# A decoder layer with attention, a long convolution and routed experts: the convolution by blocks of 128, and expert rows kept in a region per expert

## The chip, the cores and the metric

The kernel runs on one core of one Trainium2 chip. The metric is the device time of one execution in microseconds (us). Three runs of the kernel before took 780.53, 782.09 and 788.21 us; the median is 782.09. The profile comes from one execution whose page gives a span (first to last instruction) of 786.9 us and no other time.

## The reference

`x` is 4 batches of 512 tokens by 128 values. Three parts follow one another, each added to its input and normalised over the 128 values (mean and variance, no scale):

1. **Attention**: 16 heads of 8 values, 4 key and value heads, RMS norm and rotary turn of q and k, scores capped by `50*tanh(s/50)`, causal softmax, output projection.
2. **Cross attention, convolution, feed-forward**: a softmax over 32 context rows gives `c_t`; from it come scales and shifts. The scaled, normalised input goes through `s4d`, a causal convolution over 512 positions, one kernel `K[d, 0..511]` per value (by FFT of length 1024 in the reference), plus `x*D_skip`. Then a second scale and shift, a norm, a feed-forward of 512 hidden values with exact GELU, and a norm.
3. **Experts**: `gates = x @ rW + rb`; the 2 best of 8 experts are taken per token, weighted by a softmax over the two gates; each expert is `gelu(x @ W1 + b1) @ W2 + b2` with 512 hidden values. Two shared experts run on all tokens and are averaged. `out = norm(x + shared + sum_e w_e * y_e)`.

Everything is float32 and the output is (4, 512, 128).

## The kernel before, in words

**The order.** Every engine walks the same written order. `iterate` has 7 iterations `i`, each of 8 head pairs `p`, each of 6 slots `n`. In iterations 0 to 3 the slots hold the score products of batch `i` (`fill`), with the value products and the copy of their result (`close`, `oT`) at the end of a pair, and the token products (`tokens`) in its third slot. Into these slots `STEPS` puts the steps of earlier batches: `(after, p, n, name)` runs at pair `p`, slot `n` of iteration `b + after`. So batch 0's cross attention runs in iteration 1, its convolution's inverse part and feed-forward in iteration 2, its norm, gates, ranks and row numbers in iteration 3. `ONCE` holds steps that run once (convolution taps and their transform). `UNIT_AT` puts the first 43 expert units into iterations 4 to 6; the rest (`moe`) follows. An engine that waits in one step holds up all that stands behind it in its order.

**Convolution.** The taps K (`kld`) and the input `xn` are 4 tiles of 128 positions. `dft(b, n)`, n = 0 to 7, multiplies them by parts of 512x512 cosine and sine tables (`cosm`, `sin_fwd`), four products of 128x128 a step, into `ring_u`. `spectrum` multiplies by the taps' spectrum (`kc`, `ks`, `kcn`) on VectorE, six operations. `conv(b, n)`, n = 0 to 7, goes back with `cosm` and `sin_inv` into `bank_d`. `kernel_dft` does the forward transform of the taps, 8 steps. `dft` 0 to 6 stand in pairs 6 and 7 of iteration b+1, the rest in iteration b+2.

**Experts.** Two groups of two batches. A group has at most 23 blocks of 128 rows (`NB`), each block of one expert. `route` picks the two experts of a token, `rank` and `place` number its rows: `place` of a group's second batch runs `block_table` (expert of each block) and then `rows_of` for all 1,024 tokens. `copy_rows` on GpSimd writes each token's x twice into `x_rows`, beside its destination and its weight. `scatter` on GpSimd issues 16 indirect DMAs that put these rows of 130 values at their block rows in `expert_rows`, which was cleared from `blank` (1,560 KB a group; the clearing stands on SyncE's queue behind the packing of the expert weights into `expert_pack`). On GpSimd the roots of norms (`power`, L1063) stand in the same order.

**Units.** `UNITS` is 16 shared units (batches 0, 1), 23 blocks, 16 shared (batches 2, 3), 23 blocks. For a block, SyncE (`load_block`) reads the block's expert from `table`, loads 514 KB of weights (`w_blk`), `b2_blk`, and, once the output of the block that had the slot was sent (`y_sent`), its rows `x_blk`; there are 6 slots. TensorE transposes the rows (L546), does 4 products up (L850), ScalarE four GELUs (L1013), TensorE 4 products down (L880) and the bias b2 as a product (L881); VectorE weighs the rows (`weigh`, L1672), and GpSimd scatters them to `token_pairs` (L1161, `unit`), two rows per token. `final(b)` adds a batch's pairs (loaded by `load_pair`, 512 KB) to `acc`, and norms; finals 0 and 1 stand among the blocks of group 1, finals 2 and 3 at the end. `store` writes the output.

## Time and profile before

| | us |
|---|---|
| median of three runs | 782.09 (780.53 to 788.21) |
| span of the profiled execution | 786.9 |
| TensorE busy (products / weight loads) | 566.9 / 404.0 |
| VectorE, ScalarE, GpSimd busy | 363.1, 338.1, 251.2 |
| share of the chain that ended last | TensorE 44%, VectorE 23%, GpSimd 7%, transfers 7%, ScalarE 7%, issue 7%, SyncE's queue 5% |

The span less the median is 4.8 us, so a sum made on the trace is read against 786.9. Busy time alone says little here, since the limits change from stage to stage: iterations 1 to 3 begin near 140, 239 and 331 us, iteration 4 near 430; group 1's blocks run from 684.8 to 764.0 us. The idle time in front of an operation, with the operation that ended it, tells which engine is late at that place. In the names, PE is TensorE, DVE VectorE, ACT ScalarE, POOL GpSimd, SPq SyncE's queue.

### The profile page before, as it was taken

The numbers are of one execution on the slowest core, as the hardware profiler recorded it, in microseconds if no ns is written. First come the engines' busy times: TensorE is split into PE (matmuls) and PEld (weight loads), VectorE is DVE, ScalarE is ACT, GpSimd is POOL, SyncE is SP. The second block draws the span as 40 slices with busy tenths as digits, with TensorE's granted clock in tenths as the row PEclk, the third lists the DMA queues.
The fourth block names the chain that finished last, engine by engine and source line by source line (L and its number), as shares of the span: only waits on it lengthen the run. The fifth ranks groups of instructions, "written<-read, shape, count | busy, mean of one in ns | idle before, by whom it ended". The sixth has DMA issues, their size and how long they took to land.

```text
span 786.9 us, 10406 instructions
## 1 busy us (share of the span) xinstructions
PE 566.9 (72%) x3665; PEld 404.0 (51%) x3665; DVE 363.1 (46%) x1067; ACT 338.1 (43%) x565; POOL 251.2 (32%) x296
## 2 busy tenths in 40 slices
PE   2654552678788869878699882996987696987770
PEld 2213431455355633656436752765874675776660
DVE  4869279616673465645624571226321240133113
ACT  1186574565737556654475140330322242322220
POOL 3204047202351254311613147113322437033231
PEclk9955665689897989987589996999878788969895
DMA  4400000395000000000000102532161402656632
GB/s 125 147 1 1 1 1 0 82 170 195 1 1 1 15 1 0 1 1 1 1 0 1 55 14 69 154 102 67 39 188 43 135 21 100 190 143 182 200 94 80
DMA packets 37763, 51.60 MB, mean 66 GB/s; under 512 B 7097, under 2 KB 27362, under 8 KB 37442
## 3 DMA queue, kind: packets, MB, share of 16 engines
q1 hardware_dynamic: 35218, 45.82, 20.9%
q0 software_dynamic: 2496, 5.15, 1.8%
q8 instruction: 29, 0.48, 0.3%
q14 instruction: 20, 0.16, 0.1%
HBM read 41.28 MB, written 13.86 MB: 70 GB/s over the span
## 4 chain that ended last, share of the span: by engine, by line
PE 44%; DVE 23%; POOL 7%; DMA 7%; ACT 7%; issue 7%; SPq 5%; POOLq 0%; DVEq 0%; ACTq 0%
SPq L427 5%; PE ring_s L850 4%; PE bank_d L760 4%; PE bank_o L880 3%; PE bank_m L682 3%; PE ring_s L652 3%; PE ring_u L747 3%; PE bank_o L866 3%; PE ring_s L844 2%; DMA token_pairs<-y_blk,x_blk 2%; PE bank_o L669 2%; DMA x_blk<-expert_rows 2%; POOL expert_rows L1150 2%; PE bank_r L546 2%; PE ring_u L739 2%
## 5 line engine op out<-in xcount | busy, mean ns | idle before, releaser
L958 ACT ACTIVATE probs<-ring_s 128x512 f32<-128x512 f32 (+1 forms) x192 | 95.5, 524 | 118.6 <-PE ring_s L652 116.9
L1100 POOL TENSOR_SCALAR_AFFINE_SELECT probs<-probs 128x256 f32<-128x256 f32 (+1 forms) x96 | 51.6, 570 | 178.7 <-ACT probs L964 178.7
L652 PE MATMUL ring_s<-qT,kT 64*128 64x128 bf16 (+3 forms) x256 | 64.2, 350 | 49.4 <-ACT probs L958 37.8
L1013 ACT ACTIVATE g_ring<-ring_s,w_blk 128x128 f32<-128x128 f32 x184 | 52.5, 370 | 104.4 <-PE ring_s L850 95.4
L1161 POOL DMA_INDIRECT token_pairs<-y_blk,x_blk x46 | 45.6, 991 | 143.9 <-DVE y_blk L1672 143.1
L964 ACT ACTIVATE probs<-probs 128x2560 f32<-128x2560 f32 x32 | 74.8, 2337 | 0.8
L652 PEld LDWEIGHTS ring_s<-qT,kT 64*128 64x128 bf16 x256 | 16.4, 97 | 93.4 <-ACT probs L958 58.6
L850 PE MATMUL ring_s<-xT_blk,w_blk 128*128 128x128 f32 x368 | 57.0, 305 | 4.3 <-DVE xT_blk L1665 2.6
L682 PE MATMUL bank_m<-pair_sum,oT 128*128 128x64 f32 x256 | 44.0, 327 | 22.2 <-DVE oT L1467 22.2
L1063 POOL TENSOR_TENSOR rstd<-var_eps,neg_half 128x4 f32<-128x4 f32 x24 | 24.9, 1036 | 100.5 <-DVE var_eps L1394 100.4
L850 PEld LDWEIGHTS ring_s<-xT_blk,w_blk 128*128 128x128 f32 x368 | 53.4, 222 | 6.8 <-issue 4.3
L682 PEld LDWEIGHTS bank_m<-pair_sum,oT 128*128 128x128 f32 x256 | 39.2, 234 | 30.6 <-DVE oT L1467 25.5
L866 PEld LDWEIGHTS bank_o<-w_sh,g_ring 128*128 128x128 f32 x256 | 35.4, 203 | 35.7 <-issue 34.9
L669 PE MATMUL bank_o<-probs,vv 128*32 128x256 f32 (+3 forms) x512 | 52.4, 538 | 0.4 <-POOL probs L1100 0.4
L866 PE MATMUL bank_o<-w_sh,g_ring 128*128 128x128 f32 x256 | 36.0, 286 | 20.2 <-DVE acc L1678 14.0
L1009 ACT ACTIVATE g_ring<-ring_s,vcols 128x512 f32<-128x512 f32 x32 | 21.8, 688 | 66.6 <-PE ring_s L844 50.5
L1672 DVE TENSOR_SCALAR y_blk<-bank_o,x_blk 128x128 f32<-128x128 f32 x35 | 12.3, 350 | 70.8 <-PE bank_o L881 70.8
L880 PE MATMUL bank_o<-w_blk,g_ring 128*128 128x128 f32 x280 | 43.4, 306 | 0.8 <-DVE y_blk L1672 0.8
L1466 DVE COPY oT<-bank_o 64x512 f32<-64x512 f32 x32 | 21.8, 680 | 45.3 <-PE bank_o L669 45.3
L880 PEld LDWEIGHTS bank_o<-w_blk,g_ring 128*128 128x128 f32 x280 | 40.3, 221 | 2.2 <-ACT g_ring L1013 1.6
L1150 POOL DMA_INDIRECT expert_rows<-x_rows,rows_i x32 | 31.0, 969 | 18.8 <-DVE gmax L1657 9.6
L844 PE MATMUL ring_s<-x2T,w_sh 128*128 128x512 f32 x64 | 36.4, 656 | 0.8 <-ACT g_ring L1009 0.8
(356 smaller groups left out, 1076.8 us busy)
## 6 DMA issues: line engine op xcount, KB each, us to landing
w_blk<-expert_pack SPq DMA_DIRECT2D x46, 514.0 KB
expert_pack<-in_L_ffn_W SPq DMA_DIRECT2D x16, 256.0 KB
expert_rows<-blank SPq DMA_DIRECT2D x2, 1560.0 KB, 10.5
x_blk<-expert_rows SPq DMA_DIRECT2D x46, 65.0 KB
y_pair<-token_pairs SPq DMA_DIRECT2D x4, 512.0 KB
x_in<-in_x SPq DMA_DIRECT2D x4, 256.0 KB, 2.9
cosm<-in_c_cos SPq DMA_DIRECT2D x1, 1024.0 KB, 6.8
sin_fwd<-in_c_sin_fwd SPq DMA_DIRECT2D x1, 1024.0 KB, 9.4
```

Source lines behind the costliest of these rows:

```text
L652: last = mm(bank[:, c:c + w], kT[64 * r:64 * r + 64, p // 2, P * j:P * (j + 1)], qT[64 * r:64 * r + 64, p, P * j:SEQ], start=True, stop=True)
L669: last = mm(bank_o[32 * s:32 * s + 32, P * j:SEQ], vv[:, j, p // 2, :], probs[:, p % 2, c:c + SEQ - P * j], start=start, stop=not start)
L682: last = mm(bank_m[:, c:c + 64], oT[:, p % 2, P * j:P * (j + 1)], pair_sum[:, :], start=True, stop=True)
L844: last = mm(bank[:, :], w_sh[:, e, P * n:P * (n + 1)], x2T[:, of, :], start=True, stop=True)
L850: last = mm(bank[:, P * n:P * (n + 1)], w_blk[:, k % SLOTS, P * n:P * (n + 1)], xT_blk[:, k % RING, :], start=True, stop=True)
L866: last = mm(bank_o[:, P * j:P * (j + 1)], g[:, P * j:P * (j + 1)], w_sh[:, e, HID + P * n:HID + P * (n + 1)], start=(c == 0 and j == 0), s ...
L880: mm(dst, g[:, P * n:P * (n + 1)], w_blk[:, k % SLOTS, HID + HC + P * n:HID + HC + P * (n + 1)], start=(n == 0), stop=False)
L958: f(probs[:, p % 2, BASE[n]:BASE[n] + WIDTH[n]], ring_s[k % 2][:, 0:WIDTH[n]], ACT.Tanh, scale=1.0 / (CAP * float(np.sqrt(np.float32(HD))) ...
L964: f(probs[:, p % 2, :], probs[:, p % 2, :], ACT.Exp, scale=CAP).then_inc(exp_done, 1)
L1013: last = f(g_ring[:, s % RING, P * n:P * (n + 1)], ring_s[s % 2][:, P * n:P * (n + 1)], ACT.Gelu, bias=w_blk[:, k % SLOTS, HID + n:HID + n ...
L1100: last = g.affine_select(out=v, in_=v, compare_op=ALU.is_ge, fill=0.0, base=0, pattern=[[0, v.shape[1]], [1, P]], channel_multiplier=-1)
L1150: g.indirect_dma_start(out=rows_dram, out_offset=bass.IndirectOffsetOnAxis(ap=rows_i[:, k, j:j + 1], axis=0), in_=x_rows[:, k, j, :], in_o ...
```

## The change

**Convolution.** The 1024-point transform over 512 positions becomes a transform of length 256 over each tile of 128 positions, in three streams of 128 frequencies: `conv_tab` has 3 forward and 3 inverse tables of 128x128, made on VectorE (`conv_tables`). `dft(b, n)`, n = 0 to 2, is one product of a table with all four tiles (512 columns). `lags(b, n)` multiplies a stream on VectorE by the taps' transform at lags of 0 to 3 tiles and sums. `conv(b, n)` is one product of 512 columns. `spectra` builds the taps' three streams, `kernel_dft` has 2 steps.

**Experts.** A region of 1,024 rows per expert and group (`CAPACITY`), so a row number needs no block table: `rows_of` runs for every batch, and its 8 scatters (rows of 128 values, straight from `x2`) follow at once. All regions are cleared, 4.6 MB a group, from 4 KB of zeros a partition, now before the taps are stored. Weights and destinations stay in SBUF (`w_sel`, `y_rows`); b2 is packed as 128 equal rows behind the weights and added on VectorE. Block outputs are stored plainly from SyncE, in the loop that loads blocks; SyncE reads the source row of a block from `source`. `fetch` on GpSimd gathers each token's two rows by 8 indirect DMAs a batch, and `final` adds them weighted by 8 operations.

```diff
@@ STEPS, ONCE
-    (2, 0, 0, "dft", 7), (2, 0, 1, "spectrum"), (3, 0, 5, "x2_norm"), (3, 1, 0, "x2"), (2, 1, 0, "conv", 0),
-    (2, 1, 1, "conv", 1), (2, 1, 2, "conv", 2), (2, 1, 3, "conv", 3), (2, 1, 4, "conv", 4), (2, 1, 5, "conv", 5),
-    (2, 2, 0, "conv", 6), (2, 2, 1, "conv", 7), (3, 1, 1, "x2T"), (3, 1, 3, "gates"), (1, 1, 4, "yT"),
+    (3, 0, 5, "x2_norm"), (3, 1, 0, "x2"), (2, 1, 0, "conv", 0), (2, 1, 2, "conv", 1), (2, 1, 4, "conv", 2),
+    (3, 1, 1, "x2T"), (3, 1, 3, "gates"), (1, 1, 4, "yT"),
-    (1, 6, 5, "dft", 0), (1, 7, 0, "dft", 1), (1, 7, 1, "dft", 2), (1, 7, 2, "dft", 3), (1, 7, 3, "dft", 4),
-    (1, 7, 4, "dft", 5), (1, 7, 5, "dft", 6), (2, 7, 0, "ff_out"), (2, 7, 1, "ffT"), (2, 7, 5, "ff_norm"),
+    (1, 6, 5, "dft", 0), (1, 7, 1, "dft", 1), (1, 7, 2, "lags", 0), (1, 7, 3, "dft", 2), (1, 7, 4, "lags", 1),
+    (1, 7, 5, "lags", 2), (2, 7, 0, "ff_out"), (2, 7, 1, "ffT"), (2, 7, 5, "ff_norm"),
...
+            sp.wait_ge(blank_ready, 1)
+            for g in range(GROUPS):
+                at = g * GROUP_ROWS
+                load(rows_dram[at:at + NE * CAPACITY, :].rearrange("(p n r) w -> p n (r w)", p=P, r=ZERO_ROWS),
+                     zero_rows[:, :].unsqueeze(1).broadcast_to([P, NE * CAPACITY // (P * ZERO_ROWS), ZERO_ROWS * D]), blanked)
...
             sp.wait_ge(kij_ready, 1)
...
+                load(pack[e, :, B2_AT:PACK], t["L0_ffn_b2"][e].partition_broadcast(P), ld_pack)
...
                 if k >= SLOTS:
                     sp.wait_ge(u_down, BLOCKS[k - SLOTS] + 1)
+                    sp.wait_ge(y_ready_blk, k - SLOTS + 1)
                 e = sp.value_load(table[0:1, g, q:q + 1], min_val=0, max_val=NE - 1)
                 load(w_blk[:, k % SLOTS, :], pack_dram[bass.ds(e * P, P), :], w_landed[k % SLOTS])
-                load(b2_blk[0:1, k % SLOTS, :], t["L0_ffn_b2"][bass.ds(e, 1), :], w_landed[k % SLOTS])
-                if k >= SLOTS:
-                    sp.wait_ge(y_sent[k % SLOTS], 16 * (k // SLOTS))
-                at = g * GROUP_ROWS + q * P
-                load(x_blk[:, k % SLOTS, :], rows_dram[at:at + P, :], xs_landed[k % SLOTS])
+                at = sp.value_load(source[0:1, g, q:q + 1], min_val=0, max_val=GROUPS * GROUP_ROWS - P)
+                load(x_blk[:, k % SLOTS, :], rows_dram[bass.ds(at, P), :], xs_landed[k % SLOTS])
+
+            def store_block(k):
+
+                g, q = divmod(k, NB)
+                sp.wait_ge(y_ready_blk, k + 1)
+                load(y_dram[g][P * q:P * (q + 1), :], y_blk[:, k % SLOTS, :], y_sent[k % SLOTS])
...
+                for q in range(NB + SLOTS):
                     k = g * NB + q
...
+                    if q >= SLOTS:
+                        store_block(k - SLOTS)
+                    if q < NB:
+                        load_block(k)
+                        if k in STORE_BEFORE:
+                            store(STORE_BEFORE[k])
...
             def dft(b, n):
-                f, c = divmod(n, NT)
+
                 if n == 0:
                     pe.wait_ge(xmod_ready, b + 1)
-                mat = (cosm, sin_fwd)[f]
-                for j in range(NT):
-                    last = mm(ring_u[f][:, P * c:P * (c + 1)], mat[:, j, P * c:P * (c + 1)], xn[:, j, :],
-                              start=(j == 0), stop=(j == NT - 1))
-                if c == NT - 1:
-                    last.then_inc(u_full, 1)
+                k = b * U_FILLS + U_DFT + n
+                pe.wait_ge(u_free, k - 1)
+                mm(ring_u[k % 2][:, :], conv_tab[:, n, :], xn[:, :, :].rearrange("p j d -> p (j d)"),
+                   start=True, stop=True).then_inc(u_full, 1)
 
             def conv(b, n):
...
+                last = mm(bank_d[:, :], conv_tab[:, NSTREAM + n, :], spec[:, n, :, :].rearrange("p j d -> p (j d)"),
+                          start=(n == 0), stop=(n == NSTREAM - 1))
...
                     for n in range(HC):
-                        mm(dst, g[:, P * n:P * (n + 1)], w_blk[:, k % SLOTS, HID + HC + P * n:HID + HC + P * (n + 1)], start=(n == 0), stop=False)
-                    last = mm(dst, ones2[0:1, :], b2_blk[0:1, k % SLOTS, :], start=False, stop=True)
+                        last = mm(dst, g[:, P * n:P * (n + 1)], w_blk[:, k % SLOTS, HID + HC + P * n:HID + HC + P * (n + 1)],
+                                  start=(n == 0), stop=(n == HC - 1))
...
             def scatter(b):
 
-                if b % GB < GB - 1:
-                    return
-                pool.wait_ge(blanked, 16 * (b // GB + 1))
-                pool.wait_ge(rows_ready, b // GB + 1)
-                for j in range(GB * NT):
+                pool.wait_ge(blanked, 32 * (b // GB + 1))
+                pool.wait_ge(rows_ready, b + 1)
+                for j in range(NT):
                     for k in range(2):
...
+            def fetch(b):
+
+                if b % GB == 0:
+                    pool.wait_ge(y_rows_ready, b // GB + 1)
+                    for n in range(SLOTS):
+                        pool.wait_ge(y_sent[n], 16 * len(range(n, (b // GB + 1) * NB, SLOTS)))
+                if b >= 2:
+                    pool.wait_ge(pair_used, b - 1)
+                for j in range(NT):
+                    for k in range(2):
+                        g.indirect_dma_start(out=y_pair[:, b % 2, j, k, :], out_offset=None, in_=y_dram[b // GB],
+                                             in_offset=bass.IndirectOffsetOnAxis(ap=y_rows[:, k, b * NT + j:b * NT + j + 1], axis=0)).then_inc(pair_landed[b % 2], 16)
...
-            for s in range(EARLY, POSITIONS):
-                unit(s)
-                if s in FINAL_AT:
+            for of in range(GROUPS):
+                for b in range(GB * of, GB * (of + 1)):
+                    fetch(b)
+                for b in range(GB):
                     power()
...
+            def lags(b, n):
+
+                k = b * U_FILLS + U_DFT + n
+                dve.wait_ge(u_full, k + 1)
+                x = ring_u[k % 2][:, :].rearrange("p (j d) -> p j d", j=NT)
+                part = (fb, kc, ks)
+                for m in range(1, NT):
+                    op(tt(part[m - 1][:, m:NT, :], x[:, 0:NT - m, :], taps_f[:, n, m:m + 1, :].broadcast_to([P, NT - m, D]), ALU.mult))
+                tt(spec[:, n, :, :], x, taps_f[:, n, 0:1, :].broadcast_to([P, NT, D]), ALU.mult).then_inc(u_free, 1)
+                then()
+                dve.wait_ge(u_free, k + 1)
+                one(tt(spec[:, n, 1:NT, :], spec[:, n, 1:NT, :], fb[:, 1:NT, :], ALU.add))
+                one(tt(spec[:, n, 2:NT, :], spec[:, n, 2:NT, :], kc[:, 2:NT, :], ALU.add))
+                tt(spec[:, n, 3:NT, :], spec[:, n, 3:NT, :], ks[:, 3:NT, :], ALU.add).then_inc(spec_ready, 1)
...
+                dve.wait_ge(rank_read, b + 1)
+                rows_of(b)
                 if b % GB == GB - 1:
-                    dve.wait_ge(rank_read, b + 1)
                     block_table(b // GB)
-                    rows_of(b // GB)
...
-                ts(y_blk[:, k % SLOTS, :], down_bank(k)[:, 0:D],
-                   x_blk[:, k % SLOTS, D + 1:D + 2], None, ALU.mult).then_inc(y_ready_blk, 1)
+                tt(y_blk[:, k % SLOTS, :], down_bank(k)[:, 0:D], w_blk[:, k % SLOTS, B2_AT:PACK], ALU.add).then_inc(y_ready_blk, 1)
...
             def final(b):
...
+                for k in range(2):
+                    for j in range(NT):
+                        last = stt(out=a[:, j, :], in0=y_pair[:, b % 2, j, k, :], scalar=w_sel[:, k, b * NT + j:b * NT + j + 1],
+                                   in1=a[:, j, :], op0=ALU.mult, op1=ALU.add)
```

## Rows read from the trace of the kernel before

**Rows 1.** busy time of each engine by stretch: length, engines, PEclk, DMA share, GB/s
```profile
239.00:331.00 92.00, 76.12 (x502) 47.05 (x500) 49.94 (x146) 56.42 (x76) 32.32 (x45) 0.91 0.01 4
...
690.00:768.00 78.00, 58.99 (x380) 52.10 (x378) 19.53 (x70) 21.74 (x76) 23.77 (x24) 0.86 0.52 155
```

**Rows 2.** TensorE timeline: start, us, what, [idle before <-releaser]
```profile
308.60 1.02 PE L789 MATMUL bank_d<-g_raw,wt 128*128 128x512 f32 x2
...
318.98 1.16 PE L747 MATMUL ring_u<-xn,cosm 128*128 128x128 f32 x8
...
323.22 1.10 PE L682 MATMUL bank_m<-pair_sum,oT 128*128 128x64 f32 x8 [0.91 <-DVE oT L1467]
...
356.77 2.07 PE L760 MATMUL bank_d<-spec,cosm 128*128 128x128 f32 x8
```

**Rows 3.** VectorE timeline around the end of iteration 2
```profile
317.43 0.28 DVE L1445 TENSOR_TENSOR qkv<-qkv,k_parts 128x128 f32<-128x128 f32 x1
...
338.25 0.69 DVE L1539 TENSOR_TENSOR spec<-ring_u,kc 128x512 f32<-128x512 f32 x1 [6.42 <-PE ring_u L747]
```

**Rows 4.** groups of instructions, VectorE: count, busy us, mean ns, idle before
```profile
L1594 DVE TENSOR_TENSOR fb<-gates 128x256 f32<-128x256 f32 x4 | 1.7, 418 | 0.0
```

**Rows 5.** SyncE queue and the chain of waits near 183 us
```profile
153.01 21.26 SPq L427 DMA_DIRECT2D expert_pack<-in_L_ffn_W  x16
...
179.19 3.82 SPq L427 DMA_DIRECT2D expert_rows<-blank  x2
...
183.06 10.25 DMA x_in<-in_x
...
193.36 0.66 PE L546 MATMUL ring_s<-ident,x_in 128*128 128x128 f32 x4 [0.91 <-DMA x_in<-in_x]
```

**Rows 6.** POOL, VectorE and TensorE timelines in iteration 4
```profile
462.72 0.23 DVE L1642 SCALAR_TENSOR_TENSOR from_last<-row,chosen_g 128x64 f32<-128x64 f32 x1
...
466.02 1.22 POOL L1150 DMA_INDIRECT expert_rows<-x_rows,rows_i  x1 [5.03 <-DVE gmax L1657]
...
485.26 0.96 POOL L1150 DMA_INDIRECT expert_rows<-x_rows,rows_i  x1 [0.30 <-issue]
...
487.34 1.11 DVE L1401 TENSOR_SCALAR xn<-x,mean_var,rstd 128x128 f32<-128x128 f32 x4 [18.68 <-POOL rstd L1063]
...
490.59 2.05 PE L866 MATMUL bank_o<-w_sh,g_ring 128*128 128x128 f32 x8 [14.02 <-DVE acc L1678]
```

**Rows 7.** POOL timeline in iteration 3, and TensorE after it
```profile
375.51 1.36 POOL L1100 TENSOR_SCALAR_AFFINE_SELECT probs<-probs 128x512 f32<-128x512 f32 x3
382.46 1.02 POOL L1063 TENSOR_TENSOR rstd<-var_eps,neg_half 128x4 f32<-128x4 f32 x1 [5.58 <-DVE var_eps L1394]
...
387.27 1.97 PE L682 MATMUL bank_m<-pair_sum,oT 128*128 128x64 f32 x8 [1.57 <-DVE oT L1467]
```

**Rows 8.** SyncE queue timeline, first loads of group 0
```profile
493.99 0.34 SPq L427 DMA_DIRECT2D x_blk<-expert_rows  x1
495.26 0.34 SPq L427 DMA_DIRECT2D w_blk<-expert_pack  x1
```

**Rows 9.** chain that ended last, in the blocks of group 1
```profile
734.02 4.06 DMA token_pairs<-y_blk,x_blk
...
742.00 0.33 SPq L427
...
742.84 3.71 DMA x_blk<-expert_rows
```

**Rows 10.** groups of instructions: TensorE's bias product of the blocks
```profile
L881 PE MATMUL bank_o<-b_blk,ones 1*128 1x128 f32 x70 | 18.5, 346 | 0.0
```

**Rows 11.** chain that ended last, the end of the program
```profile
764.67 2.22 DMA token_pairs<-y_blk,x_blk
...
767.09 3.90 DMA y_pair<-token_pairs
771.01 0.70 DVE acc L1692
```

More of the change, by code:

```diff
@@ L488, in _ @@
             load(sb2_rows[:, :], t["L0_ffn_sb2"], ld_pack)
-            sp.wait_ge(blank_ready, 1)
-            for g in range(GROUPS):
-                load(rows_dram[g * GROUP_ROWS:(g + 1) * GROUP_ROWS, :].rearrange("(p r) w -> p (r w)", p=P),
-                     blank[:, :, :].rearrange("p r w -> p (r w)"), blanked)
             for b in range(2, B):
```

271 lines of the change are left out of this document (132 added, 139 removed).

## The prediction

> **What bounds the kernel now.** I read first the slices and the busy time by stretch, then the chain of waits, then the timelines of single engines where that chain changes engine. In the stretch of iteration 2 TensorE is busy for 76 of 92 us and no other engine for more than 56 [rows 1]: there the order written out for TensorE sets the time. In the last block stretch it is busy for 59 of 78 us, and the chain runs through transfers, not through an engine [rows 1, 9]. Three other places matter: batch 2's input arrives late behind the weight packing on SyncE's queue [rows 5], sixteen scatter issues on GpSimd hold up everything in iteration 4 [rows 6], and the end of the program is a string of transfers and norms [rows 11]. The sum is made against the one profiled execution. Its page gives no time but the span, 786.9 us, which is 4.8 above the median of the three runs (782.1); I take 4.8 off at the end.
>
> **Convolution, TensorE.** A transform step is now four products of 128 columns (eight passes, the x8 in a row): 1.16 us at full clock, 2.07 at the low one [rows 2]. A new step is one product of 512 columns, the shape of L789: 1.02 us [rows 2]. So a step costs the same, and the forward steps fall from 8 to 3, the inverse ones from 8 to 3, the one-time transform of the taps from 8 to 2. Removed per batch: 5 + 5 steps of about 1.1 us, 11 us at full clock; once: 6 steps, 6.6 us.
>
> **Convolution, VectorE.** The spectrum step is six operations of 512 elements, 0.69 us each and some 0.6 apart, about 4.0 us [rows 3]. Each of three lag steps has four products and three sums of 512 or fewer elements. By 0.69 at 512, 0.42 at 256 and 0.28 at 128 [rows 3, 4], and so 0.56 at 384, the products cost 1.95, the sums 1.26; a step is 3.1 us with its overlaps, all three 9.3, against 4.0. They sit in pair 7, before ff_norm and before the oT copies, and the third forward product waits until the first lag step has read its bank. The cover before was 6.42 us of idle VectorE in front of the spectrum [rows 3], but in pair 7 it was already late for TensorE by 0.91 us [rows 2]. Walking the order through: the third product waits some 2.3 us, and the oT copy needed by the next iteration's first token product ends at about 338.3 where that product started at 338.5. So the **forward part gives nothing** between iterations 2, 3 and 4; only at the end of iteration 1, with no feed-forward of an earlier batch beside it, it gives 3 us. The **inverse part** gives its 5 steps where TensorE is full: 5.5 us in iteration 2, 7 in iteration 3, where part of them ran at the low clock [rows 2]. In iterations 4 and 5 no attention covers the lag steps: the x2 of the batch before comes 5 to 6 us later, which takes back the steps removed there: 0. Taps: batch 2's x_in is TensorE's limit at 193.3 [rows 5]. It lands 10.25 us after its issue because 3.1 MB of blank rows (3.82 us of issue) stand ahead of it. These move to the front of the queue; eight bias copies join the packing, each at least a quarter of the mean packing issue of 21.26/16 = 1.33 us, at most all of it, so 2.7 to 10.6; I take 4, their bytes being a fourth of a weight half's. x_in lands at about 188, and six fewer steps let TensorE be there: **-5**. Convolution in all: -5 - 3 - 5.5 - 7 = -20.5; bounds -6 (all but x_in lost) and -50 (each removed step counts).
>
> **Zero fill and loads.** 9.3 MB of zeros go out before 147 us, when the taps' store is next on the queue and the DMA engines have nothing else; 2.5 MB of tables go. At the 144 to 195 GB/s of the page's slices 9.3 MB is 48 to 65 us, over by 95. I take 0; without that cover it would be up to 10 us on the taps' store.
>
> **Scatter.** Sixteen issues stand 1.265 us apart, 466.02 to 486.22, and the root of a norm waits behind them; VectorE idles 18.7 us, TensorE 14.0 [rows 6]. Now each batch scatters eight, ready 4 us earlier since the block table comes after the row numbers: 460 + 10.1 = 470. But place grows: four more table operations, five for the moved starts per half, and the index operations on one batch at a time, some 14 at 0.2 us [rows 6] = 2.8 us in front of scores and norm. The root is ready at 472.4, xn starts near 472.7 instead of 487.3. Late next are those norms themselves, with 1 to 2 us: **-13**. In exchange batch 0 scatters in iteration 3: 376.9 to 387.0 on GpSimd, where the root of x_norm ran at 382.46 [rows 7]. The mask before it is done by 376.9 and the next pair's is not yet due, the root has no slack: +4.6, and +1.4 for place: **+6**. In iterations 5 and 6 the eight issues lie beside block work: 0. The two copies of x2 into x_rows go (1.2 us of GpSimd per batch), covered both ways.
>
> **Blocks.** The bias product, L881, goes: 0.41 us of a block's 2.46 at full clock (70 passes in this bank [rows 10], 22 in the other). Where TensorE sets the pace (about 16 blocks of group 0 and the first six of group 1) that is -9. For the other 17 the pace is a loop: block k's rows load into the slot of k-6, whose output comes three positions earlier. Before: output, POOL issue and scatter 4.06, x issue, 1.9 landing, or behind a weight load 4.6 from that load's issue (742.00 to 746.55) [rows 9]. Sum 7.35, and with a block's 2.46 of products three periods are 9.8: 3.27 each. Adding two finals of 4.4 us to 17 x 3.27 + 6 x 2.46 gives 79.2, and the trace has 684.8 to 764.0. Now: output add and semaphore 0.65, store issue 0.4, the table value 0.93 (the gap of SyncE from 494.33 to 495.26 [rows 8]), w issue to x landing 4.9 with 64 KB more; 6.9 + 2.05 = 9.0: 3.0 each. SyncE alone needs 0.93 + 0.33 + 0.93 (a second value) + 0.34 + 0.45 = 3.0. I take 3.06: **-3.5**. A final has eight operations of 0.3 for two of 0.69, +1.3 each: **+2.6**.
>
> **The end.** Before: the last scatter 2.22, pair loads 3.90, then sums [rows 11]. Now a plain store (0.45 issue, about 2.3 landing), sixteen gathers on GpSimd and only then the root of final(2). No row has a gather; the scatter's 1.265 us spacing bounds it from above if issue is all, and the 991 ns of busy time from below with no gap: 15.9 to 20.2, and 24 if reading is slower. I take 20.2, the same kind of instruction. From output to the end: 2.8 + 20.2 + 1.05 + 1.1 + 2.8 + 1.5 + 1.1 + 1.1 + 5 = 36.7 against 22.3: **+14.5**.
>
> The Trainium skill's page DMA: Bandwidth & Descriptors (section Anatomy of one DMA) fits a transfer issued by GpSimd as 2.0 us plus its bytes over 436 GB/s. If sixteen gathers of 64 KB paid that one after the other, its figures give an estimate of 34.4 us instead of my 20.2. The sixteen scatters do not queue up like that [rows 6].
>
> **Sum.** -20.5 - 13 + 6 - 9 - 3.5 + 2.6 + 14.5 = -23. I give back 1.5 for low-clock stretches after new short waits: 765.5 of span, minus 4.8: **761 us**.
>
> **Rivals.** (A) The forecast, 748 to 775 by the unknown costs, 56%. (B) TensorE's steps count nearly in full, since work behind it shifts too: 25 us more, 736. For it: 76 of 92 us busy [rows 1]. Against it: VectorE was already the releaser in pair 7 [rows 2]. 17%. (C) The lag steps and smaller gaps stall TensorE and leave it at the low clock, where a step costs 2.07 for 1.16 [rows 2]; six such stretches of 3 us and the inverse gain of iteration 3 gone are 25 us less 5: about 781, no change. 14%. (D) **Slower**: SyncE's block loop becomes the bound. Its one queue now takes output stores between loads, each waiting for an output, then two values from SBUF in series. If that loop is 4.1 instead of 3.06 us, some 30 blocks cost 31 us: 792. It decides from 3.9 us per block on. For it: the queue idles 0.93 per value [rows 8] and loads wait out their slot [rows 9]. Against: its terms add up to 3.0, and it loses the wait for the scatter. 13%.
>
> The same page (section SWDGE vs HWDGE vs iDMA) calls transfers issued by SyncE the faster kind. That favours the stores, and speaks against the gathers.
>
> **Numbers.** About 1% is what runs of this kernel can tell: 774 to 790 is no change. Faster: nearly all of A and B, 0.71; same: C and the edges of A and D, 0.17; slower 0.12. The range 738 to 785 leaves out half of B and most of D.
>
> **What would show it.** Right: L747's heir takes 12 rows of 512 columns a kernel; VectorE waits for a root at most 9 us in iteration 4, but some 5 in iteration 3; blocks of group 1 come every 3.0 to 3.2 us with SyncE never idle; 16 gathers stand 1.27 us apart at the end, with some 36 us from last output to the end. Wrong: TensorE's idle in pair 7 absent (B), PEclk below 0.75 in iterations 2 and 3 (C), w_blk releasing TensorE with periods above 3.9 (D), or gathers far from 1.27 us apart.

## The result, and the profile after

The changed kernel takes **792.5 us** (median of four runs, 792.3 to 795.8) against 783.5 for the kernel before on the same chip: ratio 1.0168, interval 1.0116 to 1.0220, 1.7% slower. The forecast was 761 (738 to 785), faster. Its profiled execution took 795.8, span 793.8. Medians here are over all runs of a kernel, ratios and their intervals only over its runs that are not slowed by a lower granted clock.

That is not the whole result. Measured again, word for word, the same kernel took 791.0 and 789.2 us on two chips (1.0115, interval 0.9952 to 1.0277, and 1.0126, 1.0058 to 1.0195) and **766.8 us** on another, the fourth chip in what follows, where its ratio is **0.9751** (0.9679 to 0.9823). The kernel before stood at 781 to 788 on all of them. The record names no chip for the first measurement, so it may have been one of the two that gave 791.0 and 789.2.

The table cuts the spans at the start of named TensorE products: the first score product of iteration 2, that of iteration 3, the first shared product (L840), the first block product (L846), the first shared product of batch 2, the first block product of group 1, the end of the last product down.

| stretch, us | before | after | after, fourth chip | forecast change |
|---|---|---|---|---|
| up to iteration 2 | 244.4 | 245.4 | 250.3 | -8 |
| iteration 2 | 92.3 | 88.2 | 90.3 | -5.5 |
| iteration 3, to the first shared product | 114.9 | 125.5 | 114.1 | -7 +6 |
| to the first block | 53.7 | 44.3 | 40.7 | -13 |
| to the shared expert of batch 2 | 133.4 | 129.1 | 128.8 | -6.6 |
| to the first block of group 1 | 41.1 | 54.4 | 31.7 | 0 |
| blocks of group 1 | 83.8 | 71.4 | 73.2 | -3.4 |
| last product to the end | 23.3 | 35.4 | 35.5 | +14.5 |
| span | 786.9 | 793.8 | 764.4 | -23, 1.5 given back |

One stretch, the one before the first block of group 1, holds 22.7 of the 29.4 us between the two executions of the same kernel. Busy time by stretch, columns as in [rows 1], of after:

```profile
239.00:331.00 92.00, 69.29 (x408) 34.46 (x408) 58.57 (x170) 59.85 (x81) 29.44 (x42) 0.85 0.01 4
331.00:423.00 92.00, 68.71 (x328) 33.67 (x325) 42.88 (x134) 47.59 (x65) 34.03 (x44) 0.74 0.02 6
423.00:465.00 42.00, 26.80 (x110) 15.32 (x110) 24.86 (x85) 7.94 (x11) 8.90 (x11) 0.61 0.08 26
...
600.00:690.00 90.00, 62.99 (x368) 48.87 (x367) 21.81 (x100) 26.64 (x60) 28.82 (x29) 0.83 0.34 99
690.00:768.00 78.00, 49.77 (x388) 46.50 (x386) 21.67 (x86) 25.06 (x88) 7.23 (x8) 0.92 0.58 174
```

Against [rows 1] TensorE is busy for 69 instead of 76 us in iteration 2 and for 50 instead of 59 in the last blocks: its work has gone. From 423 to 465 its granted clock is 0.61. From 600 to 690 something else stands in the way. The waits of after name it (engine, line, releaser: us in total, times, longest):

```profile
DVE acc L1701 <- remote: 29.2, 1, 29.2
ACT g_ring L1005 <- remote: 27.6, 4, 19.1
DVE y_blk L1696 <- remote: 6.7, 1, 6.7
```

"Remote" is a release that the trace doesn't show. Timelines of GpSimd, ScalarE, VectorE, TensorE and SyncE in that stretch of after:

```profile
640.52 1.06 POOL L1135 DMA_INDIRECT expert_rows<-x,rows_i  x1 [21.54 <-DVE rows_i L1673]
...
650.77 1.00 POOL L1148 DMA_INDIRECT y_pair<-expert_out,y_rows  x1 [0.30 <-issue]
...
669.57 0.94 POOL L1148 DMA_INDIRECT y_pair<-expert_out,y_rows  x1 [0.30 <-issue]
...
654.16 0.69 ACT L1005 ACTIVATE g_ring<-ring_s,vcols 128x512 f32<-128x512 f32 x1 [5.74 <-remote]
673.92 0.69 ACT L1005 ACTIVATE g_ring<-ring_s,vcols 128x512 f32<-128x512 f32 x1 [19.08 <-remote]
...
674.91 0.69 DVE L1701 SCALAR_TENSOR_TENSOR acc<-bank_o,x 128x512 f32<-128x512 f32 x1 [29.16 <-remote]
...
658.61 2.32 PE L867 MATMUL bank_o<-sb_rows,ones 2*128 2x128 f32 x8
674.66 2.07 PE L840 MATMUL ring_s<-x2T,w_sh 128*128 128x512 f32 x2 [13.74 <-ACT g_ring L1005]
...
664.06 0.71 SPq L431 DMA_DIRECT2D w_blk<-expert_pack  x1
672.47 0.69 SPq L431 DMA_DIRECT2D x_blk<-expert_rows  x1
```

GpSimd issues the eight scatters of batch 3 and, with no pause, the sixteen gathers of batches 0 and 1: 24 issues in one string, 640.5 to 670.5. ScalarE has its input at 657.0 (L840 is done) and runs at 673.9; VectorE has its bank at 660.9 and runs at 674.9; SyncE needs 8.4 us between two loads. All three go on 2.0 to 4.4 us after the last issue has ended. So the parts of their idle time in which the input was there are 17.0 us of ScalarE's 19.1 and 14.0 us of VectorE's 29.2. TensorE, which waits for them, loses 4.4 and 13.7 us. The same stretch on the fourth chip, GpSimd, ScalarE, VectorE and SyncE:

```profile
631.99 1.06 POOL L1135 DMA_INDIRECT expert_rows<-x,rows_i  x1 [21.59 <-DVE rows_i L1673]
...
661.04 0.94 POOL L1148 DMA_INDIRECT y_pair<-expert_out,y_rows  x1 [0.30 <-issue]
...
649.59 0.69 ACT L1005 ACTIVATE g_ring<-ring_s,vcols 128x512 f32<-128x512 f32 x1 [1.06 <-PE ring_s L840]
651.34 0.69 ACT L1005 ACTIVATE g_ring<-ring_s,vcols 128x512 f32<-128x512 f32 x1 [1.06 <-PE ring_s L840]
...
644.86 0.69 DVE L1701 SCALAR_TENSOR_TENSOR acc<-bank_o,x 128x512 f32<-128x512 f32 x1 [7.64 <-PE bank_o L867]
...
648.61 0.34 SPq L431 DMA_DIRECT2D w_blk<-expert_pack  x1
649.72 0.34 SPq L431 DMA_DIRECT2D x_blk<-expert_rows  x1
```

The same 24 issues at the same pace, and nobody waits: ScalarE every 1.75 us, loads 1.1 us apart.

### The profile page after: what moved, and what is told of

Its sections match the earlier page's. It is cut to its first block, busy times and chain, and to the rows that moved or that the text cites. A ratio compares the mean times of both kernels' runs of the same rounds, so it can differ in the third digit from the quotient of the medians.

```text
span 793.8 us, 9514 instructions
## 1 busy us (share of the span) xinstructions
PE 511.0 (64%) x3049; PEld 328.0 (41%) x3049; DVE 399.0 (50%) x1216; ACT 336.7 (42%) x565; POOL 228.8 (29%) x281
## 4 chain that ended last, share of the span: by engine, by line
PE 43%; DVE 25%; ACT 9%; POOL 8%; issue 6%; another core or an unknown queue 4%; DMA 3%; SPq 2%; POOLq 0%; DVEq 0%; ACTq 0%
PE bank_o L862 4%; PE bank_o L670 4%; PE ring_s L846 4%; PE ring_s L840 3%; PE ring_s L653 3%; PE bank_o L876 3%; PE bank_m L683 3%; PE bank_d L756 2%; DMA x_blk<-expert_rows 2%; PE ring_u L741 2%; PE bank_r L552 2%; POOL y_pair L1148 2%; ACT qT L947 2%; ACT probs L954 2%
## 5 line engine op out<-in xcount | busy, mean ns | idle before, releaser
L653 PE MATMUL ring_s<-qT,kT 64*128 64x512 bf16 (+3 forms) x256 | 62.0, 355 | 49.3 <-ACT probs L954 36.5
L683 PE MATMUL bank_m<-pair_sum,oT 128*128 128x64 f32 x256 | 44.0, 327 | 34.4 <-DVE oT L1474 34.4
L670 PE MATMUL bank_o<-probs,vv 128*32 128x256 f32 (+3 forms) x512 | 59.9, 602 | 2.6 <-POOL probs L1096 2.6
L846 PE MATMUL ring_s<-xT_blk,w_blk 128*128 128x128 f32 x368 | 54.5, 296 | 6.7 <-DVE xT_blk L1689 5.0
L846 PEld LDWEIGHTS ring_s<-xT_blk,w_blk 128*128 128x128 f32 x368 | 50.0, 211 | 9.6 <-issue 7.4
L840 PE MATMUL ring_s<-x2T,w_sh 128*128 128x512 f32 x64 | 38.8, 695 | 21.6 <-ACT g_ring L1005 21.6
L1005 ACT ACTIVATE g_ring<-ring_s,vcols 128x512 f32<-128x512 f32 x32 | 21.9, 687 | 67.3 <-PE ring_s L840 38.5
L1148 POOL DMA_INDIRECT y_pair<-expert_out,y_rows x32 | 30.5, 953 | 51.7 <-issue 51.7
L876 PE MATMUL bank_o<-w_blk,g_ring 128*128 128x128 f32 x280 | 40.7, 293 | 5.6 <-DVE y_blk L1696 5.6
L1135 POOL DMA_INDIRECT expert_rows<-x,rows_i x32 | 31.3, 978 | 34.1 <-DVE rows_i L1673 25.5
L670 PEld LDWEIGHTS bank_o<-probs,vv 128*32 128x32 f32 x512 | 25.2, 137 | 37.5 <-issue 30.5
L1696 DVE TENSOR_TENSOR y_blk<-bank_o,w_blk 128x128 f32<-128x128 f32 x35 | 10.2, 291 | 54.5 <-PE bank_o L876 47.7
```

What stands on the lines that cost most here:

```text
L653: last = mm(bank[:, c:c + w], kT[64 * r:64 * r + 64, p // 2, P * j:P * (j + 1)], qT[64 * r:64 * r + 64, p, P * j:SEQ], start=True, stop=True)
L670: last = mm(bank_o[32 * s:32 * s + 32, P * j:SEQ], vv[:, j, p // 2, :], probs[:, p % 2, c:c + SEQ - P * j], start=start, stop=not start)
L683: last = mm(bank_m[:, c:c + 64], oT[:, p % 2, P * j:P * (j + 1)], pair_sum[:, :], start=True, stop=True)
L840: last = mm(bank[:, :], w_sh[:, e, P * n:P * (n + 1)], x2T[:, of, :], start=True, stop=True)
L846: last = mm(bank[:, P * n:P * (n + 1)], w_blk[:, k % SLOTS, P * n:P * (n + 1)], xT_blk[:, k % RING, :], start=True, stop=True)
L876: last = mm(dst, g[:, P * n:P * (n + 1)], w_blk[:, k % SLOTS, HID + HC + P * n:HID + HC + P * (n + 1)], start=(n == 0), stop=(n == HC - 1))
```

## The experiments

Kernels of one group ran on one chip with the kernel before; other groups ran on other chips. "Stalls" below are idle stretches marked remote.

**1. The two parts alone, and the gathers moved.** conv_only and experts_only take one part of the change each (experts_only has a 2 KB pad in SBUF for the layout).

```
 fetch_paced:  for each gather of batches 0 and 1
+                  pool.wait_ge(u_down, BLOCKS[NB] - 25 + 3 * (8 * b + 2 * j + k) // 2)
 fetch_late:   before the first gather of batch 0
+                  pool.wait_ge(u_down, BLOCKS[NB] + 3)
-FINAL_AT = {BLOCKS[NB] + 4: 0, BLOCKS[NB] + 9: 1}
+FINAL_AT = {BLOCKS[NB] + 15: 0, BLOCKS[NB] + 18: 1}
+STORE_BEFORE = {NB + 20: 0, NB + 22: 1}
```

> The kernel before with the convolution part of the change alone (one product of 512 columns per step, lag steps on VectorE). Theory 1, the gain is real but is eaten by TensorE's low clock and by the later x2 in iteration 4: within 5 us of the kernel before, 779 to 788 us, with PEclk below 0.80 in the stretch 423 to 465. Theory 2, the convolution keeps most of what was forecast and the expert part loses it: 765 to 772 us, PEclk as before (0.82).

> The kernel before with the expert part alone (regions, stores, gathers, bias in SBUF), old convolution. Theory 1: end +13, the stall at the gathers of group 0 some +12, scatter in iteration 3 +6, against scatter relief in iteration 4 -10 and the blocks of group 1 -11: sum +10, about 793 us. Theory 2 (the expert part alone loses what the convolution wins): 800 us or more.

> The changed kernel, but each of the sixteen gathers of batches 0 and 1 waits until TensorE has finished one and a half more units of the shared expert, so they are spread over some 40 us and leave the scatter of batch 3 alone. Theory 1, an unbroken string of indirect issues on GpSimd holds up ScalarE and VectorE: the idle stretch of TensorE near 652 to 674 us shrinks from 18 us to under 6, and the time falls by 10 to 14 us to about 780. Theory 2, each indirect issue costs the other engines the same wherever it stands: the stall is spread, the time stays within 3 us of 792.5.

> The changed kernel, but the sixteen gathers of batches 0 and 1 wait for the third block of group 1 and then run in one string beside the blocks; the finals of batches 0 and 1 and their stores stand eleven and nine positions later. Theory 1, string of issues stalls whoever runs beside it: the stall at 652 to 674 goes down to the 6 to 8 us that the scatter alone makes, and a new one of 5 to 15 us stands among the blocks, at SyncE's loads or ScalarE: 785 to 795 us. Theory 2, the stall at 652 to 674 has another cause than the gathers: it stays at 18 us of idle TensorE.

Measured, with 785.9 for before: conv_only **792.1** (1.0097, 1.003 to 1.0164), experts_only **759.3** (0.9687, 0.9622 to 0.9752), fetch_paced 762.8 (0.9725), fetch_late 764.8 (0.9757). No trace of the four has a stall. Both my theories on the expert part were wrong: alone it wins 26.5 us. fetch_paced is 30 us faster than the first measurement of the changed kernel, but not for the reason expected: its GpSimd still issues 24 in one string, 627.6 to 657.6. The waits were met already. In fetch_late there was no stall for a later string to remove either, so on this chip neither of its theories is tested. conv_only wins nothing, as theory 1 had it, and lies 4 us above the 788 that theory 1 allowed. Its stretches:

```profile
239.00:331.00 92.00, 73.67 (x417) 37.52 (x416) 57.70 (x167) 58.12 (x79) 29.79 (x42) 0.82 0.01 4
331.00:423.00 92.00, 71.00 (x383) 35.12 (x384) 49.39 (x153) 54.33 (x75) 28.91 (x40) 0.77 0.00 1
423.00:465.00 42.00, 30.23 (x132) 19.08 (x125) 25.80 (x93) 8.36 (x10) 10.93 (x12) 0.61 0.09 26
```

**2. The same kernel again, one instruction more, a shifted stream, and TensorE filled up.**

```
 one_wait:     before the first gather of batch 0
+                  pool.wait_ge(u_down, BLOCKS[NB] - 25)
 dve_shift:    at VectorE's start
+            for _ in range(16):
+                one(v.memset(held[:, :], 0.0))
 conv_filled:  the first inverse product four times more, the real ones after it
+    (2, 1, 0, "again"), (2, 1, 1, "again"), (2, 1, 2, "again"), (2, 1, 3, "again"),
+    (2, 1, 4, "conv", 0), (2, 1, 5, "conv", 1), (2, 2, 0, "conv", 2),
```

> The changed kernel itself, word for word, once more, beside kernels that differ from it by a few instructions. In the trace the kernel with waits in front of the gathers still issues its gathers 1.25 us apart in one string, so its waits took nothing away, and yet it was 30 us faster. Theory 1, the long stalls of ScalarE, VectorE and SyncE during GpSimd's string belong to the changed kernel as it was built: 789 to 796 us again. Theory 2, they belong to the first measurement: 760 to 770 us now.

> The changed kernel with a single wait more, on GpSimd before the first gather of batch 0, for a count of TensorE that has been reached before the scatter of batch 3 is out. Theory 1, the stall hangs on how the instruction streams lie and not on the pace of the gathers: one instruction may be enough, 760 to 770 us. Theory 2, each of the sixteen waits gave the other engines a gap to run in: 788 to 795 us.

> The changed kernel with sixteen small fills of one table on VectorE at its start (about 2 us of work before the first input lands), so that every later instruction of VectorE stands sixteen or more places further on. Theory 1, a stall comes when an engine needs new instructions while GpSimd issues in one string: the stalls of VectorE move or go, 760 to 795 us but not the same places (572, 646). Theory 2, placement has no part in it: the stalls stand at the same two instructions with the same lengths, 6.7 and 29.2 us, and the time is 792.

> The changed kernel with the first inverse product of each batch issued four more times ahead of the real ones (the same bank is filled again), so TensorE has 7 inverse products where the kernel before had 8 steps. Theory 1, TensorE's steps are worth less than the clock they keep up: PEclk in 239 to 465 rises from 0.77 by 0.03 or more, first shared unit within 3 us of the changed kernel's or earlier. Theory 2, TensorE's time in iterations 2 to 4 goes by its number of steps: the first shared unit comes 8 to 13 us later.

Measured, with 788.0 for before: after_again **791.0**, one_wait 794.0, dve_shift 794.7, conv_filled 802.4. All four stall at the same instructions: VectorE for 6.3 to 6.8 us at the scatter of batch 2, ScalarE and VectorE until 4 us after the 24th issue. One wait does not cure it and sixteen places in VectorE's stream don't move it, so where VectorE's instructions lie is not the cause. conv_filled: the clock of its iterations 2 and 3 is 0.85 and 0.78 against 0.82 and 0.70 in after_again's trace, and its first shared product starts at 454.8, not at 457.7, with twelve products more in front of it; but its median is 11 us above after_again's. The trace, taken in the fastest of its four runs, shows 4 us of that, all of it late: the blocks of group 1 take 77.3 us, not 72.2. Those 3 us of gain are less than the spread, since with the same instructions up to there the first shared product starts anywhere from 450.3 to 459.1. So one trace shows that twelve more products made it no later than in its fellows, where theory 2 wanted 8 to 13 us; that filling pays is not shown.

**3. Kernel or chip.** after_third is the changed kernel, fetch_paced_2 and experts_only_2 repeat group 1.

```
 spaced:       for each gather of batches 0 and 1
+                  pool.wait_ge(u_down, BLOCKS[NB] + 8 * b + 2 * j + k)
               for each scatter of batch 3
+                  pool.wait_ge(u_down, BLOCKS[NB] - 30 + 2 * (2 * j + k))
+FINAL_AT = {BLOCKS[NB] + 21: 0, BLOCKS[NB] + 23: 1}
+STORE_BEFORE = {NB + 21: 0, NB + 22: 1}
```

> The changed kernel a third time, now on one chip with kernels whose traces showed no stall. Twice it stood at 791 to 793 us with ScalarE, VectorE and SyncE idle beside GpSimd's string of 24 issues; the kernels with and without that stall were so far measured on two different chips. Theory 1, the stall belongs to the kernel: 788 to 796 us with 12 us or more of idle TensorE in the stretch of the 24 issues. Theory 2, it belongs to the chip: the same as fetch_paced_2 of this job within 4 us.

> The changed kernel with sixteen waits that are already met, once more, beside the changed kernel. Theory 1 (kernel): 760 to 768 us, no idle stretch of ScalarE while GpSimd issues. Theory 2 (chip): within 4 us of the changed kernel of this job, whatever that is.

> The expert part of the change alone, once more, beside the whole change. Theory 1 (kernel): 757 to 765 us, no stall. Theory 2 (chip): if the changed kernel stalls here, this one stalls too beside its 24 issues in one string, and stands at 775 us or more.

> The changed kernel with each of the eight scatters of batch 3 held until TensorE has finished two more shared units (2.9 us apart), and each of the sixteen gathers of batches 0 and 1 until one more block of group 1 is done (some 2.9 us apart); finals and stores of these batches move to the end of the group. Theory 1, an unbroken string is what stalls the others: no stall at the scatter of batch 3, none beside the gathers, 758 to 768 us on any chip; the stall at the unspaced scatter of batch 2 (6.7 us) may stay. Theory 2, single issues stall them too, or the string has no part in it: idle ScalarE stands beside spaced issues.

Measured, with 781.4 for before: after_third **789.2**, fetch_paced_2 **780.8** (0.9987), experts_only_2 **792.6** (782.6 to 797.7; 1.0058, 0.9981 to 1.0135), spaced 786.6 (1.0077). By its ratio experts_only_2 stands near 785 us: experts_only has lost its 26.5 us, with the same instructions. Theory 2, the chip, holds for it, with a reservation: every chip was used in one session only, so a chip and the moment at which it was used can't be told apart. fetch_paced_2 is 8.4 us faster than after_third, outside the 4 us of its theory 2: TensorE, held up, now made some of its waits bind (its string was 19 issues, then pauses), and its shared stretch is 49.1 us. In spaced, GpSimd and ScalarE:

```profile
644.62 0.96 POOL L1137 DMA_INDIRECT expert_rows<-x,rows_i  x1 [0.30 <-issue]
...
680.33 0.94 POOL L1152 DMA_INDIRECT y_pair<-expert_out,y_rows  x1 [3.48 <-PE bank_d L876]
683.28 0.94 POOL L1152 DMA_INDIRECT y_pair<-expert_out,y_rows  x1 [2.02 <-PE bank_o L876]
686.20 0.94 POOL L1152 DMA_INDIRECT y_pair<-expert_out,y_rows  x1 [1.97 <-PE bank_d L876]
...
647.04 1.27 ACT L1005 ACTIVATE g_ring<-ring_s,vcols 128x512 f32<-128x512 f32 x2 [3.60 <-remote]
...
682.15 1.14 ACT L1009 ACTIVATE g_ring<-ring_s,w_blk 128x128 f32<-128x128 f32 x4 [1.81 <-PE ring_s L846]
```

The waits I put before the scatters of batch 3 were met already, so that string of eight stood, and stalled ScalarE for 3.6 us. Beside the gathers, one per finished block and 1.5 to 4.4 us apart, nothing stalls, and the shared stretch is 37.2 us instead of 54.4 in after_third. Both issue the same transfers, so on a chip that stalls it is the unbroken string, as far as one kernel shows it (the gathers now also stand beside blocks, not beside the shared expert). The trace of before agrees: its 46 scatters of block outputs, at most three in a row, stand beside blocks, and nobody stalls beside them. The 758 to 768 us of theory 1 were missed all the same. Against after_third's trace 17.2 us are gained there, and 7.3 lost before the first shared product (with the same instructions), 7.1 in the blocks of group 1 and 7.2 at the end. In the blocks the last loads wait behind the store of batch 0, and TensorE idles once:

```profile
736.96 0.48 PE L552 MATMUL bank_m<-ident,x_blk 128*128 128x128 f32 x1 [12.65 <-DMA x_blk<-expert_rows]
```

**4. Strings broken into small ones, with the new convolution, the old, and a shorter one.** The edit in all but after_fourth (the changed kernel):

```
 gathers of batches 0, 1:   if k == 0: pool.wait_ge(u_down, BLOCKS[NB] + 1 + b * NT + j)
 scatter of batch 2, j > 0: pool.wait_ge(u_down, 23 + j)
 scatter of batch 3:        pool.wait_ge(u_down, 44 + 2 * j)
+FINAL_AT = {BLOCKS[NB] + 11: 0, BLOCKS[NB] + 15: 1}
+STORE_BEFORE = {}
```

> The changed kernel on the chip of this job, as the measure for the other three. Either the stall beside the string of 24 issues is there (787 to 797 us, as on three chips) or this chip has none (760 to 768 us, as the nearly same kernel on a fourth).

> The changed kernel with the strings broken: the scatters of batches 2 and 3 and the gathers of batches 0 and 1 go out two at a time, each pair held until TensorE has finished the next block or two more shared units; finals of batches 0 and 1 seven and six positions later, their stores behind the last block's. Theory 1, only a string of more than a few issues stalls ScalarE, VectorE and SyncE: no stall over 2 us at 563 and none at 640 to 670, the shared expert of batches 2 and 3 takes 30 to 33 us instead of 54, whole kernel 758 to 768 us on any chip. Theory 2, what counts is the number of issues: the idle time of ScalarE and VectorE is spread, 780 us or more.

> The same spacing with the old convolution. Theory 1, the new convolution is worth nothing because the clock falls and VectorE's lag steps come late: within 5 us of the kernel with pairs and the new convolution, on either side. Theory 2, the new convolution costs, as it did alone (6 us over the kernel before): this one is 5 us faster or more. Theory 3, it wins what was forecast: this one is 15 us slower or more.

> The kernel with pairs, its lag steps cut to one product and one sum of 384 elements (the three products and two sums that fold earlier blocks of the sequence in are left out, so the convolution is incomplete): some 2.2 us of VectorE less per lag step, 6.6 per batch. Theory 1, VectorE's lag steps are what eats TensorE's saved steps: the first shared unit comes 10 us earlier or more (at 445 or before), the kernel is 8 to 15 us faster. Theory 2, TensorE's clock eats it: PE stays low in iterations 2 and 3 (27 and 58 us or more), and the first shared unit moves by less than 5 us.

Measured, with 784.3 for before: after_fourth **766.8** (0.9751), pairs **775.0**, experts_pairs **774.8**, lags_short **760.8**. This chip doesn't stall, so pairs could not show its cure; it shows the price, 8 us (6.8 in the traces): the scatter is later (the shared stretch is 38.7 instead of 31.7 us), and the blocks of group 1 take 76.0 instead of 73.2. With and without the new convolution the time is the same (theory 1). lags_short leaves out three products and two sums of each lag step (the sum kept has 128 elements, not 384 as written) and is 14.2 us faster than pairs: theory 1 is right in kind, the first shared product coming 7.9 us earlier (444.8 to 452.7), not 10, and 5.5 us before the earliest of the kernels with whole lag steps. Half of the 7.9 is one wait at the end of iteration 3. TensorE in pairs, and then in lags_short:

```profile
427.14 1.13 PE L749 MATMUL ring_u<-xn,conv_tab 128*128 128x512 f32 x2 [2.58 <-DVE spec L1554]
437.25 1.97 PE L683 MATMUL bank_m<-pair_sum,oT 128*128 128x64 f32 x8 [6.37 <-DVE oT L1480]
```

```profile
424.42 1.13 PE L749 MATMUL ring_u<-xn,conv_tab 128*128 128x512 f32 x2 [1.59 <-DVE spec L1552]
429.39 1.39 PE L683 MATMUL bank_m<-pair_sum,oT 128*128 128x64 f32 x8 [2.41 <-DVE oT L1480]
```

**5. The best candidate, and its string cut in two.** experts_late is experts_only with fetch_late's edit.

> The expert part of the change with the old convolution, a third time: 759 us on one chip without the stall, 793 on one with it. It is the best candidate so far. 757 to 766 us if this chip has no stall (then 2.5 to 3.5% under the kernel before), 780 to 797 if it has one.

> The same with the sixteen gathers of batches 0 and 1 held until the third block of group 1 is done, finals eleven and nine positions later, stores eight and five: two strings, of 8 and of 16 issues, in place of one of 24, the second beside blocks. Theory 1, the stall grows with a string's length and starts some 8 us into it: on a chip without the stall 2 us over its neighbour (as with the new convolution); on one with it 8 to 15 us under its neighbour. Theory 2, the second string stalls the block loop as much as it stalled the shared expert: the same as its neighbour within 4 us on a stalling chip.

Measured, with 787.3 for before: experts_only_3 **761.6** (0.9743, 0.9650 to 0.9836), experts_late 764.8 (0.9699, 0.9590 to 0.9807). No stall in either. The expert part alone wins 2.6 to 3.1% on two chips; on one that stalls it can't be told from before. experts_late has the same ratio as its neighbour within the intervals, as its theory 1 had it for a chip without the stall. No version was shown to win on a chip that stalls: pairs and experts_late never met one.

## Why the prediction was wrong

**The failed step** is "In iterations 5 and 6 the eight issues lie beside block work: 0". It was wrong in both directions, and it looked at eight issues where the program has 24 in a row. A second step failed by more, the -20.5 of the convolution: up to the first shared product the profiled run is 21.9 us behind the forecast, the shared stretch 13.3.

- *What it missed as a gain.* Before, sixteen scatters end at 670.7 and the first x_blk of group 1 waits for them. In conv_only, which has the old scatter and no stall, TensorE idles 7.69 us for that load and the stretch is 42.0 us (637.7 to 679.8); in after it is 31.7 on the chip without a stall. That is -9.4, the chain that I had priced in iteration 4 and not in 6.
- *What it missed as a cost.* Beside a string of GpSimd issues the other engines can stop: +22.7 in the shared stretch (54.4 against 31.7), and 6.7 us of VectorE at the scatter of batch 2, which hold TensorE for 4.1. The trace of before had the warning, and I did not read it:

```profile
666.37 0.69 DVE L1678 SCALAR_TENSOR_TENSOR acc<-bank_o,x 128x512 f32<-128x512 f32 x1 [16.37 <-remote]
```

There it cost nothing: the first load of group 1 could not start until the string was over anyway. The change removed that wait and made the string longer, and the stall came into the open. Rival D, the one slower case, gave 792 by another mechanism (SyncE's block loop), and this mechanism is refuted: see below. The number agreed by chance.

**Point by point.**

- *x_in, -5*: wrong. The blank rows did go to the front, but x_in was issued at 181.95, 1.1 us earlier, since its slot comes free only when batch 0's attention residual has read it. The bias copies took about 0.6 us each, near the 0.5 assumed. Its product started 3.6 us earlier (189.80 for 193.36 [rows 5]), and then ScalarE's probabilities held TensorE up:

```profile
181.95 0.38 SPq L431 DMA_DIRECT2D x_in<-in_x  x1
...
189.80 0.44 PE L552 MATMUL ring_s<-ident,x_in 128*128 128x128 f32 x2
...
195.31 2.90 PE L625 MATMUL ring_s<-wqkv,xT 128*128 128x192 f32 x8 [3.56 <-ACT probs L954]
```

- *Forward at the end of iteration 1, -3*: not there; iteration 2 starts at 245.0 to 251.6 us in the kernels with the new convolution, at 245.8 to 250.8 in those with the old one and the new expert part.
- *Lag steps*: sized right. Three took 9.5 us (320.84 to 330.30; forecast 9.3), and the third product waited 2.55 (forecast 2.3):

```profile
322.57 2.07 PE L749 MATMUL ring_u<-xn,conv_tab 128*128 128x512 f32 x2 [2.55 <-DVE spec L1548]
...
320.84 0.55 DVE L1547 TENSOR_TENSOR fb<-ring_u,taps_f 128x384 f32<-128x384 f32 x1
...
330.01 0.29 DVE L1553 TENSOR_TENSOR spec<-spec,ks 128x128 f32<-128x128 f32 x1
```

- *Inverse, -5.5 and -7*: -4.2 in iteration 2 with that forward wait in it, though the other traces with the same instructions have 87.7 to 92.2 us there, before 92.3; in conv_only iteration 3 is 8.4 us shorter up to its last pair. Then it is given back: from that pair to the first shared product before needs 31.0 us, conv_only 37.3. I had set the later x2 against the steps removed in iterations 4 and 5. What costs is its start: no later attention work hides the oT copy, which queues behind the lag steps (6.37 us of TensorE in pairs, 2.41 in lags_short), and the stretch 423 to 465 runs at a granted clock of 0.61. So the convolution is worth **0** (pairs against experts_pairs) to +6 (conv_only), not -20.5; after_third against experts_only_2 lies between, 0.7% by the ratios. Rival C (14%) named the clock; it is there, and it is not refuted: lags_short, 14 us faster than pairs, has 78 us at the low level from iteration 2 to the first shared product, pairs 99, before 61. Shortening the lag steps also gave back 20 us of full clock, so that run shows what the lag steps cost in all, with the low clock that goes with them, and doesn't separate the two.
- *Zero fill, 0*: nothing waits for it.
- *Scatter, -13 and +6*: eight issues from 470.8 (forecast 460), roots right behind them:

```profile
381.78 1.05 POOL L1059 TENSOR_TENSOR rstd<-var_eps,neg_half 128x4 f32<-128x4 f32 x1
382.87 1.12 DVE L1408 TENSOR_SCALAR xn<-x,mean_var,rstd 128x128 f32<-128x128 f32 x4 [2.41 <-POOL rstd L1059]
...
481.87 1.11 DVE L1408 TENSOR_SCALAR xn<-x,mean_var,rstd 128x128 f32<-128x128 f32 x4 [2.36 <-POOL rstd L1059]
```

  VectorE's wait of 18.7 us [rows 6] is 2.4; shared product to first block is 9.3 us shorter, 13.0 on the fourth chip. In iteration 3 the root stands behind the issues as forecast, but 48.2 us after the iteration's start where [rows 7] has it at 45.7: 2.5 late, not 4.6. With the old convolution and the new expert part that stretch is 115.3 (twice) or 118.9 to 119.1 us (three times), before 114.9: +0.4 to +4.2 for the forecast +6.
- *Blocks, -9, -3.5, +2.6*: sum -9.9, measured -4.3 and -12.4, together -16.7. From block 9 to block 21 of group 1 (counted from 0) the mean period is 3.06 us, as forecast (3.22 on the fourth chip); before it is 3.73, not 3.27: that is where the surplus lies. The 7.35 us behind 3.27 can't be rebuilt from the terms given for it, and [rows 9] shows one that they lack: a scatter lands at 738.08 (734.02 + 4.06), and the x load on the chain is issued at 742.84, after 4.8 us of SyncE's own issues. No run tried it. SyncE's loop takes 2.7 us a block where it is not waiting, with 0.8 for a value: D would have needed 3.9.

```profile
725.97 0.34 SPq L431 DMA_DIRECT2D x_blk<-expert_rows  x1
726.35 0.43 SPq L431 DMA_DIRECT2D expert_out<-y_blk  x1
727.61 0.34 SPq L431 DMA_DIRECT2D w_blk<-expert_pack  x1
728.71 0.34 SPq L431 DMA_DIRECT2D x_blk<-expert_rows  x1
```

- *End, +14.5*: +12.2. Sixteen gathers 1.26 us apart take 19.9 (forecast 20.2). The page DMA: Bandwidth & Descriptors of the Trainium skill gave 34.4 if each transfer waited for the one before; they overlap, so that reading doesn't hold here. The final sums have eight operations in 2.31 us.

```profile
761.30 1.01 POOL L1148 DMA_INDIRECT y_pair<-expert_out,y_rows  x1 [42.30 <-issue]
...
780.24 0.95 POOL L1148 DMA_INDIRECT y_pair<-expert_out,y_rows  x1 [0.30 <-issue]
781.20 1.05 POOL L1059 TENSOR_TENSOR rstd<-var_eps,neg_half 128x4 f32<-128x4 f32 x1
...
783.31 2.31 DVE L1717 SCALAR_TENSOR_TENSOR acc<-y_pair,w_sel,acc 128x128 f32<-128x128 f32 x8
```

On the fourth chip the span fell by 22.5 us where I had summed 21.4. That was luck: up to the first shared product the sum was 17.4 us too good, mostly the convolution, and the scatter chain of group 1 (9.4 us), its blocks (7.2) and the end (2.3) were as much too bad.

## What to carry to other kernels

When a wait is priced in one stage, price it in every stage where the same code runs, and look at what stood hidden behind it, above all idle stretches whose releaser the profile can't name. Work taken from TensorE and given to VectorE is worth nothing where a copy that TensorE needs next queues behind it, however right the price of the work itself. A kernel with long strings of GpSimd-issued transfers should be timed on several chips, and better twice on each, before a verdict of 2% is believed, and the strings kept short where that costs nothing.

## What the runs showed of the hardware

**A stall that needs both a chip and a string.** In the first measurement and on two chips (789 to 793 us for the same code) ScalarE, VectorE and SyncE stop beside unbroken issues 1.26 us apart: an idle 0.6 to 3.6 us at most strings of eight, 4.0 to 6.8 at that of batch 2; at 24, ScalarE stops for up to 17.0 us with its input there and VectorE for 14.0. One gather per block causes none. On three other chips none of ten traces has one, the strings of 24 included. TensorE goes on until it needs the others. Why chips differ is open, and so is whether it is the chip or the moment, since each of the five was used in one session only.

One rival can be ruled out, that the three engines wait for instructions to be fetched. The page of after lists two queues of kind instruction (packets, MB, share):

```profile
q8 instruction: 25, 0.41, 0.2%
q14 instruction: 24, 0.20, 0.1%
```

The Trainium skill's page Runtime: NRT & Kernel Launch (section Instruction fetch mechanics) says that each engine fetches its instructions by a DMA queue of its own in blocks of 16 KiB, and that TensorE's store is four times as large. The trace agrees for TensorE at most: q8's packets of 16 KB go with the number of its instructions (25 packets for 6,391 recorded in after, 29 for 7,436 in experts_only), while q14's are of 8 KB. The trace has the time of each packet. In after no packet of q14 moves between 592.9 and 680.8 us, and the three engines go on at 672.5 to 674.9; on the fourth chip two of them move beside the string, at 651.7 and 654.4. A fetch that ended the stall would have to land before the engines go on. These come after: in all ten traces with a stall the next 8 KB packet moves 5 to 11 us behind the end of the last stall, and none in the 10 us before it.

**Less work, lower clock.** Taking a fifth of TensorE's passes out of iteration 2 (408 for 502) went with a lower granted clock. It is plainest from 423 to 465 us: 0.56 to 0.88 in the fourteen traces with the new convolution, 0.92 to 1.00 in the six with the old. From 239 to 331 it is 0.80 to 0.85 against 0.81 to 0.94, from 331 to 423 it is 0.70 to 0.78 against 0.76 to 0.80. So 7 us less of busy time are not 7 us less of time.
